# Segment sums from differences of running sums, and another order and engine split in the front, in a fused Mamba-2 and attention-with-experts kernel

## The reference

```python
# block A: Mamba-2, then an MLP
zxbcdt = layernorm(x) @ in_proj_w.T             # z, xBC, dt
xBC = silu(causal_conv4(xBC)); dt = softplus(dt + dt_bias)
h = h * exp(dt * A) + dt * x_t (x) B_t          # 4 heads of 64, state 64
y = rms(( h . C_t + D * x ) * silu(z)) @ out_proj_w.T
x1 = layernorm(x) + y ; a = x1 + mlp(layernorm(x1))
# block B: causal attention (16 heads of 8, rms-normed q and k), then 4 experts, top 2
x2 = layernorm(x) + attention(rms(layernorm(x))) @ wo.T
b = x2 + sum_e weight_e * expert_e(rms(x2))
out = x + a * silu(b)
```

## Time and profile before

| | us |
|---|---|
| median of 3 runs | 860.65 (860.46 to 865.01) |
| the profiled execution | 861.28 |
| its span | 859.5 |
| PE busy | 784.9 |
| VectorE busy | 618.1 |
| ScalarE busy | 498.5 |
| GpSimd busy | 320.8 |

### The profile page before, as it was taken

One profiled execution on the slowest core, in us unless ns is written; L12 is line 12 of the kernel. 1 busy time (PEld: TensorE's weight loads), 2 busy tenths in 40 slices (PEclk: granted clock), 3 DMA queues, 4 the chain that ended last, 5 costly groups with the idle time before them and its releaser, 6 DMA issues. The chain is left out here.

```text
span 859.5 us, 18101 instructions
## 1 busy us (share of the span) xinstructions
PE 784.9 (91%) x5472; PEld 482.5 (56%) x5472; DVE 618.1 (72%) x1469; ACT 498.5 (58%) x928; POOL 320.8 (37%) x600
## 2 busy tenths in 40 slices
PE   2779999998999989998999989999899998999897
PEld 1455564755557465665647555475556656475545
DVE  2786479785887768786697858877587876967534
ACT  2435784476753776457844767537764568447552
POOL 5424543053512717036340535227170362505400
PEclk9999999999999999999999999999999999999999
DMA  4000000000000000000000000000000000000000
GB/s 166 2 8 17 12 0 1 9 16 25 0 8 12 14 12 0 8 14 25 0 0 8 14 24 0 6 13 14 12 0 8 13 25 0 0 8 14 24 2 13
DMA packets 15145, 11.73 MB, mean 14 GB/s; under 512 B 1040, under 2 KB 13968, under 8 KB 14992
## 3 DMA queue, kind: packets, MB, share of 16 engines
q1 hardware_dynamic: 15120, 11.43, 4.4%
HBM read 7.76 MB, written 2.10 MB: 11 GB/s over the span
## 5 line engine op out<-in xcount | busy, mean ns | idle before, releaser
L1102 ACT ACTIVATE sb_pr<-S 128x768 f32<-128x768 f32 (+1 forms) x192 | 161.2, 878 | 135.0 <-PE S L445 134.9
L1198 DVE TENSOR_REDUCE sb_mx<-S 128x2 f32<-128x256 f32 (+3 forms) x256 | 198.0, 818 | 32.8 <-PE S L445 31.6
L1722 POOL TENSOR_SCALAR_AFFINE_SELECT sb_pr<-sb_pr 128x256 f32<-128x256 f32 (+1 forms) x192 | 98.8, 520 | 301.7 <-ACT sb_pr L1102 301.0
L445 PE MATMUL R<-sb_pr,sb_va 128*32 128x512 f32 (+3 forms) x1024 | 89.7, 445 | 6.3 <-POOL sb_pr L1722 6.3
L445 PE MATMUL R<-sb_W,sb_pr 128*128 128x96 f32 (+1 forms) x512 | 69.5, 276 | 0.0
L445 PE MATMUL R<-sb_xfT,sb_W 128*128 128x512 f32 x144 | 69.2, 602 | 0.0
L445 PE MATMUL S<-sb_kT,sb_qT 32*128 32x256 f32 (+3 forms) x512 | 56.0, 383 | 14.2 <-DVE sb_mx L1198 10.7
L445 PEld LDWEIGHTS R<-sb_W,sb_pr 128*128 128x128 f32 x512 | 63.5, 192 | 3.8 <-issue 3.5
L445 PEld LDWEIGHTS S<-sb_kT,sb_qT 32*128 32x128 f32 x512 | 27.4, 182 | 67.0 <-DVE sb_mx L1198 59.2
L1432 DVE SCALAR_TENSOR_TENSOR sb_x<-R,sb_wts,sb_x 128x96 f32<-128x96 f32 x128 | 40.6, 317 | 22.8 <-PE R L445 19.4
L445 PE MATMUL S<-sb_qT,sb_kT 32*128 32x256 f32 (+3 forms) x512 | 56.1, 383 | 0.5 <-ACT sb_pr L1102 0.5
(11 more groups left out here) (217 smaller groups left out, 1708.7 us busy)
## 6 DMA issues: line engine op xcount, KB each, us to landing
sb_xin<-x SPq DMA_DIRECT2D x9, 256.0 KB, 2.8
sb_W<-weights SPq DMA_DIRECT2D x1, 2290.0 KB, 11.6
sb_qT<-sb_mT SPq DMA_DIRECT2D x128, 4.0 KB
sb_xres<-x SPq DMA_DIRECT2D x8, 256.0 KB, 2.8
out<-sb_xres SPq DMA_DIRECT2D x7, 256.0 KB, 2.3
sb_cT<-sb_xact SPq DMA_DIRECT2D x8, 128.0 KB, 2.3
sb_W<-weights SPq DMA_DIRECT2D x1, 514.0 KB, 5.6
sb_cst<-consts SPq DMA_DIRECT2D x1, 328.0 KB, 3.1
```

The costliest lines, as they stand in the source:

```text
L445: return pe.matmul(o, lhsT, rhs, start=start, stop=stop, skip_group_check=True)
L1102: act.activation(pr[:, e % 4, :, 0:n], S[pair_of_exp(e)][:, :, 0:n], ACT.Exp).then_inc(p_sb, 1)
L1198: o = dve.tensor_reduce(mx[:, n // P - 1, g, heads[0]:heads[1] + 1], found[:, :, at_col:at_col + n], AX.X, ALU.max, negate=True)
L1722: pool.affine_select(out=keep, in_=keep, compare_op=ALU.is_ge, fill=0.0, base=0, pattern=pattern, channel_multiplier=-1)\
```

## The change

The segment sums are taken as a difference of running sums. VectorE splits the running sums (the first 16 columns of `cumulate`) into a rounded part and the remainder (`sums_in_parts`, into `cs`), PE turns `cs` once a round (`turn_sums`), ScalarE makes the right side `seg_v` and four left sides `seg_l` from it with scales and biases of ones, minus ones and zeros, and GpSimd spreads `seg_v` over the heads (`seg_r`, one product a round). A segment is then one fp32r pass over `seg_l`, `seg_r` and one bf16 pass that adds -1e30 to the future (`maskb`, `identb`). `decays` and `rs` go; `h2a` gets its own buffer.

In the front the first qkv projection moves to the end of `stage_a`, the second ahead of `op`, and the third and fourth behind the transposes of `ao`. VectorE copies v out of PSUM (`evac_values`), ScalarE only q and k. `x1n` and `xf` are made by GpSimd (`first_norm`, `second_norm`). PE turns `xf` directly ahead of the q and k tokens and takes the gate logits in the middle of them; the gate's operations on VectorE stand between the second and third copy of `kT`, and ScalarE's start of the convolution stands behind the copies of `qT`. The tile statistics, constants and the order of the copies follow from this.

```diff
             def segments(r, c):
 
-                pe.wait_ge(rs_sb, at(rs_sb, r, c + 1))
+                pe.wait_ge(segl_sb, at(segl_sb, r, 1 + T))
+                pe.wait_ge(segr_sb, at(segr_sb, r, 1))
...
-                mm(R[1][:, :], after, rs[:, c % 2].rearrange("p h t -> p (h t)")).then_inc(seg_ps, 1)
+                mm(R[1][:, :], seg_l[:, c, :], seg_r[:].rearrange("p h t -> p (h t)"), True, False)
+                mm(R[1][:, :].rearrange("p (h t) -> p h t", h=NH), maskb[:],
+                   identb[:].unsqueeze(1).broadcast_to([P, NH, P]), False, True).then_inc(seg_ps, 1)
...
+            def turn_sums(r):
+                pe.wait_ge(cs_sb, at(cs_sb, r, 2))
+                pe.wait_ge(act_up, at(act_up, r, 17))
+                pe.transpose(R[1][:, 0:P], cs[:].rearrange("p c k -> p (c k)"), ident).then_inc(csT_ps, 1)
...
+            def turn_second_norm(r):
+                pe.wait_ge(xf_sb, at(xf_sb, r, 1))
+                transposes(R[0], lambda t: xf[:, t, :]).then_inc(xfT_ps, 1)
...
                     for n in range(2 * G):
+                        if tail and n == 0:
+                            turn_second_norm(r)
+                        if tail and n == T:
+                            gate(r)
                         if n == 0:
                             pe.wait_ge(lo_sb, at(lo_sb, r, 1))
...
                 weigh_values(r, G * UNITS - 2)
+                pe.wait_ge(xbT_sb, at(xbT_sb, r, 1))
+                pe.wait_ge(p_sb, at(p_sb, r, G * UNITS))
+                project_qkv(r, 0)
                 turn_y(r, T - 1)
```

ScalarE in `stage_a`, behind the first exponential:

```diff
+                    if e == 0:
+                        act.wait_ge(csT_ps, at(csT_ps, r, 1))
+                        act.wait_ge(segr_sb, at(segr_sb, r, 0))
+                        act.activation(seg_v[:], R[1][:, 0:P], ACT.Identity, bias=seg_sums[:, 1:2],
+                                       scale=seg_sums[:, 0:1]).then_inc(segl_sb, 1)
+                        act.wait_ge(seg_ps, at(seg_ps, r, 0))
+                        for c in range(T):
+                            act.activation(seg_l[:, c, :], R[1][:, 0:P], ACT.Identity, bias=seg_low[:, c:c + 1],
+                                           scale=seg_high[:, c:c + 1]).then_inc(segl_sb, 1)
```

VectorE:

```diff
+            def evac_values(r, ts_):
...
+                for t in ts_:
+                    dve.wait_ge(qk_sb, at(qk_sb, r, t + 1))
+                    ts(va[:, t, :, 0:HD], bank(t)[:, 2 * D:3 * D].rearrange("p (h d) -> p h d", h=AH),
+                       ratio[:, t:t + 1], None, ALU.mult).then_inc(qkv_sb, 1)
...
+            def sums_in_parts(r):
+
+                total = S[0][:, 0, 0:T * NH].rearrange("p (c h) -> p c h", h=NH).unsqueeze(2)\
+                    .broadcast_to([P, T, 2, NH])
+                parts = cs[:, :, 0:16].rearrange("p c (x y h) -> p c x y h", x=2, y=2)
+                dve.wait_ge(dec_sb, at(dec_sb, r, 1))
+                dve.wait_ge(csT_ps, at(csT_ps, r, 0))
+                dve.tensor_copy(parts[:, :, :, 0].bitcast(F32R), total).then_inc(cs_sb, 1)
+                dve.wait_ge(cs_sb, at(cs_sb, r, 1))
+                tt(parts[:, :, :, 1], total, parts[:, :, :, 0], ALU.subtract).then_inc(cs_sb, 1)
```

GpSimd (`second_norm` stands behind the weight product on q, `first_norm` ahead of it):

```diff
+            def first_norm(r):
+                pool.wait_ge(r2_sb, at(r2_sb, r, 2))
...
+                for t in range(T):
+                    i = ts(x1n[:, t, :], x1[:, t, :], mv2[:, t, 0:1], r2[:, 1, t:t + 1],
+                           ALU.subtract, ALU.mult)
+                i.then_inc(x1n_sb, 1)
...
+            def second_norm(r):
+                pool.wait_ge(r3_sb, at(r3_sb, r, 2))
...
+                for t in range(T):
+                    i = ts(xf[:, t, :], x2[:, t, :], r3[:, 1, t:t + 1], 0.0, ALU.mult, ALU.add)
+                i.then_inc(xf_sb, 1)
...
-            def decays(r, c, tail):
-
-                pool.wait_ge(dt_sb, at(dt_sb, r, DT_STEPS))
-                if c == 0 and tail:
-                    pool.wait_ge(up_ps, at(up_ps, r, 9))
-                pool.wait_ge(seg_ps, at(seg_ps, r, c - 1))
-                tt(rs[:, c % 2], upto.unsqueeze(1).broadcast_to([P, NH, P]),
-                   dta[:, c, :].unsqueeze(2).broadcast_to([P, NH, P]), ALU.mult).then_inc(rs_sb, 1)
...
             def stage_a(r, tail):
-                decays(r, 0, tail)
+                pool.wait_ge(segl_sb, at(segl_sb, r, 1))
+                pool.sem_inc(pool_passed, 1)
+                pool.wait_ge(seg_ps, at(seg_ps, r, 0))
+                tt(seg_r[:], seg_v[:].unsqueeze(1).broadcast_to([P, NH, P]),
+                   seg_head[:].unsqueeze(2).broadcast_to([P, NH, P]), ALU.mult).then_inc(segr_sb, 1)
...
-                    if u == 5 and g < T - 1:
-                        decays(r, g + 1, tail)
```

More of the change, by code:

```diff
@@ L671, in experts_down @@
                     pe.wait_ge(h1_sb, at(h1_sb, r, 2))
+                if t == 3 and head:
+                    pe.wait_ge(segl_sb, at(segl_sb, r, 1 + T))
                 for e, (h, name) in enumerate(((h0, "e0d"), (h1, "e1d"), (h2c, "e2d"), (h3b, "e3d"))):
@@ L707, in stage_b @@
                     i.then_inc(ot3_ps, 1)
+                if head:
+                    project_qkv(r, 1)
+                if tail:
                     pe.wait_ge(yT_sb, at(yT_sb, r, 0))
@@ L1056, in stage_b @@
                             act.activation(sp[:, 2], sp[:, 1], ACT.Exp, scale=-1.0).then_inc(spe_sb, 1)
-                            if tail:
-                                gate_exp(r)
-                elif tail:
+                if head:
+                    for n in range(2):
+                        tap = V_CONVW + TAPS * n + TAPS - 1
+                        act.wait_ge(xc_sb, at(xc_sb, r, n + 1))
+                        act.wait_ge(conv_sb, at(conv_sb, r, 0))
+                        act.activation(cv[:, n], xc[:, n, TAPS - 1:TAPS - 1 + L], ACT.Identity,
+                                       bias=vec[:, V_CONVB + n:V_CONVB + n + 1],
+                                       scale=vec[:, tap:tap + 1]).then_inc(conv_act, 1)
+                if tail:
                     gate_exp(r)
@@ L1385, in stage_b @@
                        ALU.subtract).then_inc(lo_sb, 1)
-                for _ in gate:
-                    pass
+                gate = gate_logits(r) if tail else iter(())
+                if not head:
+                    for _ in gate:
+                        pass
                 if head:
@@ L1392, in stage_b @@
                         dve.tensor_copy(kT[:, g, :], bank((2 * g + 1) % 4)).then_inc(kT_sb, 1)
+                        if g == 1:
+                            for _ in gate:
+                                pass
                     dve.wait_ge(xc_sb, at(xc_sb, r, 3))
@@ L1422, in stage_b @@
                        ALU.add).then_inc(sv_sb, 1)
+                if head:
+                    sums_in_parts(r)
                 for t in range(T):
@@ L1640, in stage_b @@
                     tt(sp[:, 1], sp[:, 1], sp[:, 0], ALU.subtract).then_inc(spa_sb, 1)
+                if tail and not head:
+                    second_norm(r)
                 if tail:
                     pool.wait_ge(x1n_sb, at(x1n_sb, r, 1))
-                    pool.sem_inc(pool_passed, 1)
                     tt(x1[:], x1[:], row[:, R_B2:R_B2 + D].unsqueeze(1).broadcast_to([P, T, D]),
```

201 lines of the change are left out of this document (115 added, 86 removed).

## The result

| us | before | after |
|---|---|---|
| median of the runs | 862.83 (4 runs, 860.46 to 865.05) | 883.69 (4 runs, 880.67 to 888.52) |
| profiled execution, its span | 861.28, 859.5 | 882.48, 880.8 |
| mean granted clock of the profiled execution | 0.993 | 0.974 |

The ratio is 1.0247, with an interval of 1.0186 to 1.0309: slower, as forecast, but by 21 us and not by 5, and outside the range.

The account below looks back on a forecast made before the run. PE, busy for 91% of the span, was taken as the bound. Against the profiled 861.28 us: -8.4 - 0.4 + 1.0 + 10.5 - 0.05 + 2.9 = +5.55, so 866.8, as median 866; range 853 to 872, the forecast's own 862 to 869.

Parts of the forecast that it names:

- Front order and second norm: Front: `xf` on GpSimd ends late, so the first expert matmul comes 1.5 us later a round, 7 x 1.5 = +10.5.
- so about 0.3 for 128, at least 0.28 and at most 0.4, four of them 1.2: Front, first norm: price in us of GpSimd's 128-column `x1n` tiles, taken from rows of 16 and 512 columns.
- The second norm beside VectorE: Front: GpSimd's `xf` tiles and VectorE's casts and subtractions exclude each other; the last subtraction ends at 322.5, `xf` at 322.8.
- taken in turns: Front: four `xf` tiles of 0.3 us on GpSimd alternate with four VectorE operations of 0.65.
- The gate: Front: gate logits, about 0.95 us on PE, move between the token transposes; no cost on VectorE was forecast.
- Segment sums: Unit loop: a segment costs 0.4 to 0.86 us, taken as 0.65, which saves 0.2 four times a round.
- I count none of it: Segment saving of 0.2 us: becomes a hole in chunks 0 to 2; chunk 3's is in the unit loop term.
- Unit loop: Before unit 18: without the decay product on GpSimd PE goes on 1.2 us sooner a round; the new transpose costs 0.12.
- Clock: Front: larger PE holes bring about two more clock falls than now, 1.45 us each, +2.9.
- the second rival's mark: PE's clock row shows falls in each round; that rival, falls in most fronts, forecast 870.6 us, chance 0.13.
- Ends: Start: +0.25 for a GpSimd memset, -0.3 for V copies gone from ScalarE; last round's norms on GpSimd 0.

Follow-up runs that it names:

- Kernel 3: The changed kernel with the mean's subtraction left out of `x1n`, so its GpSimd tile multiplies and adds with one pointer; 878.04 us, ratio 1.0188.
- Kernel 9: The changed kernel with GpSimd's three convolution additions cut to 16 of 512 columns, the gate left in its place; 876.01 us, ratio 1.0123.
- kernel 6: The changed kernel with GpSimd's product of q with its weights moved ahead of the four `x1n` tiles; 883.49 us, ratio 1.0215.
- kernel 1: The kernel before with the segment sums alone changed, front order and engine split as before; 865.70 us, ratio 1.0015.
- kernel 8: The changed kernel with both norms' tiles back on VectorE and the gate's logits behind the fourth `kT` copy; 871.56 us, ratio 1.0091.
- kernel 4: The changed kernel with both norms (`x1n` and `xf`) back on VectorE, the rest as changed; 867.27 us, ratio 1.0066.

## Why the prediction was wrong

Direction and mechanism of the front held. The price of the `x1n` tiles and one step without a cost make up most of the 16 us by which it missed. By its own terms, against the profiled executions (forecast +5.55, measured +21.2): the fronts cost 6.3 more than forecast and the middles 7.4, the loops gained 1.1 less, the stretch to the first `turn_y` and the last round cost 2.3 and 1.6 more, and the separate 2.9 for the clock is already in these parts.

- **Front order and second norm, forecast +10.5; measured +16.8 in seven fronts.** The path was right: `xf` is PE's last wait. The step that failed is "so about 0.3 for 128, at least 0.28 and at most 0.4, four of them 1.2". The tiles of `x1n` took 0.79 each, 3.13 for four. Counted from `turn_y`, they began at 8.6 (forecast 8.4, which is 315.2), so `xf` began at 12.95 and not at 12.0, ended at 17.3 and not at 16.0, and the first expert matmul came at 22.2 and not at 21.3. Neither of the rows that the price came from the earlier trace rows subtracts: the one of 16 columns has constants, and the one of 512 columns, 0.77 us, multiplies and adds with two pointers. Kernel 3 shows that the form is worth 0.42 of the 0.79, and 1.5 us a front. For the form of `xf` the bound held: 0.37.
- **The second norm beside VectorE.** The exclusion was real, but "taken in turns" was kind to GpSimd: one tile took 0.37 and three took 1.33 to 1.35, 4.35 for the four where 4.0 were forecast. PE's wait for `xf` was 1.40 at most, not 3, since it had already waited 3.41 for `x1n`.
- **The gate, forecast nothing; measured +7.4.** "The gate (about 0.95, which stood before them and ran in VectorE's time)" counted the gate on PE alone. Its six VectorE operations moved as well, from ahead of GpSimd's convolution into it. This is the largest single error, and the earlier trace rows already held it: a 16-column product of 0.98 beside a GpSimd product. Kernel 9 shows it alone. The Trainium skill's page "SBUF — State Buffer", section "SBUF: two separate sides", gives the rule: a VectorE operation with two SBUF inputs and a GpSimd operation that reads SBUF exclude each other, and who starts first holds the ports to its end. The rows agree: the product at 435.41 came 0.18 into an addition and ended with it, after 1.12 us. The reduction with one input at 435.21 began just ahead of the addition, so it tests nothing.
- **Segment sums, forecast 0.65 for a segment; measured 0.63 in chunks 0 and 3, 0.70 and 0.84 in chunks 1 and 2.** Nearly right; but the fp32 matmul that they replace takes 0.95 to 1.06 from start to start, and not 0.86, so 0.4 is saved in chunks 0 and 3 and not 0.2. "I count none of it" was right for chunk 0, which waits for the maxima.
- **Unit loop, forecast -1.2 + 0.12; measured -0.90.** The sign and nearly the size were right, for partly another reason. From the segment of chunk 3 to `turn_y` it took 407.42 - 397.94 = 9.48 us before and 416.34 - 407.50 = 8.84 after: 0.43 is the shorter segment and 0.24 the shorter wait. The power began 35.9 behind `cumulate` (368.83), a little before the 36.3 to 36.8 of the forecast, but took 2.07 beside VectorE's products (1.65 at 11.01, where VectorE had nothing), and a small product behind it took 0.90 where the one before took 0.20. So the selects began at 39.5, where 38.9 to 39.2 were forecast, and the wait did not vanish.
- **Clock, forecast two falls more.** The profiled execution had one in each of the seven fronts, where the one before had it in the first alone. One of them (windows):

```profile
429.50:432.90 3.40, 2.79 (x7) 1.67 (x5) 3.24 (x5) 2.22 (x6) 3.40 (x4) 0.50 0.00 0
```

  That was the second rival's mark, and not the loss: the fall lies between the transposes of `x1n` and those of `xf`, and PE still came to the latter 1.40 us too early, in other fronts 0.15 to 1.3. It costs where that wait is gone, as in kernel 6, or where it comes later: in kernel 3 fronts with a fall took 22.1 or more and those without 20.7. And where the forecast had none, behind the segment of chunk 0, kernel 1 had one in four of seven rounds and kernel 8 in all, at 1.4 us each.
- **Ends.** The last round, forecast 0, lost 1.6 to the same `x1n` tiles: PE waited 2.76 for them there and 0.37 before. The stretch to the first `turn_y` was 1.95 longer after; kernel 4, with the same instructions there, took 104.17 against 104.31 before, so its instructions do not need it. The clock was down for 13.7 us of it after, and for 3.4 before.

## What to carry to other kernels

When operations change place or engine, follow each of them on every engine that it uses, and lay the other engine's long operations beside the new place: a product of 16 columns cost 0.17 us in one place and 1.25 in another. Price a moved operation from a row of its own form, operands and engine, and where there is none, widen the bound. And a saving on PE that turns into waiting can cost more clock than it brings; compare runs at one clock before calling an edit worthless, and try a spare matmul in the hole.

## What was not expected of the hardware

- GpSimd's tile of 128 columns took 0.79 us as subtract and multiply with two pointers, 0.37 as multiply and add with one. VectorE took 0.34 for the first.
- Beside a row of VectorE operations GpSimd got one 128-column tile in 1.33 us, 0.96 more than alone, while VectorE's casts kept 1.29 for two. In that stretch VectorE paid almost nothing.
- Two more matmul passes a round, which lengthen a segment by 0.23 us each and whose results are thrown away, took a kernel from a ratio of 1.0015 to the kernel before to one of 0.9895. Why the clock fell behind a given hole in some rounds and not in others stays open.
